# Attention heads on one core: PSUM banks dealt in the order of use, a multiplication and a split moved to other engines, two accumulators per block

## The reference, cut to what matters

```
q, k, v = the projections of the normalized input x     (scales folded into q and k)
s       = q @ k.T                      # 2048 x 2048 per head
m       = max over keys of s           # one per query, for a stable softmax
p       = exp(s - m)
o       = (p @ v) / sum over keys of p
x       = x + concat(o over heads) @ Wo + bo
```

## Time and profile before

| | before |
|---|---|
| median of 3 runs | 5179.72 us |
| the profiled execution's own time | 5180.22 us |
| its span, first to last instruction | 5178.5 us |
| PE busy | 4647.7 us (90%) |
| DVE busy | 2437.1 us (47%) |
| ACT busy | 1614.8 us (31%) |
| POOL busy | 1663.3 us (32%) |
| mean granted TensorE clock | 0.947 |
| the attention heads, first PE instruction to last DVE instruction | 1235.0 to 2225.7 us |

### The profile page before, as it was taken

How to read it: one execution, slowest core, us unless ns; L and a number is a source line. 1 busy time by engine, 2 the same in 40 slices (tenths; PEclk the granted TensorE clock), 3 DMA queues, 4 the chain that set the end, 5 groups by cost and what they waited for, 6 DMA issues and landing times. The chain is left out here.

```text
span 5178.5 us, 65784 instructions
## 1 busy us (share of the span) xinstructions
PE 4647.7 (90%) x26052; PEld 2578.8 (50%) x26052; DVE 2437.1 (47%) x3254; ACT 1614.8 (31%) x2764; POOL 1663.3 (32%) x1050
## 2 busy tenths in 40 slices
PE   6359997899999999977999869999999989789996
PEld 3124443333333333245666536666666658666663
DVE  7865888366666666852222223333333334512222
ACT  5414542212555555823111122222222220311110
POOL 2010001003888887023555401111111110145553
PEclk9679998999999999998999989999999999889998
DMA  2000000100000000026888720000000022468997
GB/s 73 0 15 7 6 0 35 35 1 1 1 1 1 1 1 1 1 96 191 259 251 260 176 99 23 31 31 31 23 31 29 23 82 84 160 190 259 259 258 196
DMA packets 237585, 417.69 MB, mean 81 GB/s; under 512 B 31472, under 2 KB 119536, under 8 KB 237296
## 3 DMA queue, kind: packets, MB, share of 16 engines
q1 hardware_dynamic: 179952, 270.89, 15.6%
q0 software_dynamic: 57344, 142.64, 11.3%
HBM read 297.53 MB, written 115.93 MB: 80 GB/s over the span
## 5 line engine op out<-in xcount | busy, mean ns | idle before, releaser
L2363 PE MATMUL linb_pr_ps<-lin_z,linb_wt 128*128 128x512 f32 x1536 | 677.7, 594 | 17.0 <-POOL linb_slope_own L2333 17.0
L1534 ACT ACTIVATE attc_prob<-attc_ps 128x512 f32<-128x512 f32 x1024 | 549.0, 596 | 425.7 <-PE attc_ps L1447 376.7
L1410 POOL TENSOR_TENSOR attc_acc<-attc_acc,attc_prob 128x2048 f32<-128x2048 f32 x144 | 651.5, 4524 | 68.7 <-ACT attc_prob L1534 51.2
L1558 DVE TENSOR_REDUCE attc_peak<-attc_ps 128x2 f32<-128x1024 f32 x384 | 469.7, 1226 | 256.6 <-PE attc_ps L1455 256.6
L1447 PE MATMUL attc_ps<-att_q,att_k 32*128 32x512 f32 x2048 | 528.6, 612 | 0.0
L2363 PEld LDWEIGHTS linb_pr_ps<-lin_z,linb_wt 128*128 128x128 f32 x1536 | 286.3, 191 | 342.5 <-issue 324.5
L1455 PE MATMUL attc_ps<-att_k,att_q 32*128 32x512 f32 x1536 | 443.6, 654 | 2.9 <-DVE attc_tot L1581 2.9
L2539 DVE SCALAR_TENSOR_TENSOR linb_gated<-linb_osb,linb_norm_w,linb_proj 128x512 f32<-128x512 f32 x64 | 94.4, 1474 | 668.1 <-ACT linb_osb L2466 668.1
L2340 POOL TENSOR_TENSOR linb_sq<-linb_osb 128x512 f32<-128x512 f32 x64 | 70.1, 1096 | 1039.6 <-ACT linb_osb L2466 1039.6
L1468 PE MATMUL attc_ps<-attc_prob,att_v 128*32 128x256 f32 (+1 forms) x3472 | 318.4, 439 | 0.3 <-ACT attc_prob L1534 0.3
L1074 DVE TENSOR_TENSOR_SCAN ssmb_state<-ssmb_decay,ssmb_bu 128x2048 f32<-128x2048 f32 x64 | 280.8, 4414 | 54.2 <-PE ssmb_y_ps L927 29.4
(11 more groups left out here) (462 smaller groups left out, 7591.0 us busy)
## 6 DMA issues: line engine op xcount, KB each, us to landing
moe1w_wgu<-in_L_ffn_gate_up_proj SPq DMA_DIRECT2D x32, 1536.0 KB
moe2w_wgu<-in_L_ffn_gate_up_proj SPq DMA_DIRECT2D x32, 1536.0 KB
moe1w_wd<-in_L_ffn_down_proj SPq DMA_DIRECT2D x32, 512.0 KB
gated_features<-linb_gated SPq DMA_DIRECT2D x64, 256.0 KB, 2.3
moe2w_wd<-in_L_ffn_down_proj SPq DMA_DIRECT2D x32, 512.0 KB
linc_gt<-gated_features SPq DMA_DIRECT2D x7, 2048.0 KB, 8.2
linb_wt<-in_L_attn_b_qkv_w SPq DMA_DIRECT2D x16, 768.0 KB, 4.6
residual_rows<-residual SPq DMA_DIRECT2D x8, 1024.0 KB, 4.3
```

The source lines that it names most:

```text
L1410: pool.tensor_tensor(acc[:, n % 2, :, :], before, prob[:, U % NP, :, :], ALU.add).then_inc(pool_done, 2 if at == 1 else 1)
L1534: nc.scalar.activation(prob[:, U % NP, h, :], ps[:, n % 3 if at < 0 else at % 6, :], ACT.Exp).then_inc(exp_done, 1)
L1558: V.tensor_reduce(peak[:, w // TT % 2, i % QH, 2 * hp:2 * hp + 2, b], ps[:, bank:bank + 2, :], axis=AX.X, op=ALU.max).then_inc(mx_used, 1)
L2363: last = nc.tensor.matmul(pr_ps[:, use % 2, :], wt[:, b, kind, k, :], z[:, k, t * NB:(t + 1) * NB], start=(k == 0), stop=(k == DT - 1))
```

## The change

All of it is in `attention_heads`:

- The banks 0 to 6 become one ring of seven. A planning loop numbers every use (a score, the maximum of one head, the sums, the rows) in the order in which PE comes to it, and records which semaphore count says that it is read. Use number x takes bank x mod 7 and waits for the release of use x - 7.
- Maxima are reduced head by head: four reductions of 128 x 512 a unit in place of two of 128 x 1024.
- The sums leave PSUM by an ACT copy into `tot` (two slots now); DVE takes the reciprocal in SBUF in four quarters of 128 columns, one in each of four successive units; the multiplication into `q` is done by POOL, after the addition of unit 6 of the next block.
- The split of the maxima: DVE only negates and reduces; ACT writes the high part, POOL subtracts for the low part.
- The accumulator of a block becomes two, for units 0 to 6 and units 7 to 13, in a ring of three. Units 0 and 1, and 7 and 8, are added together, so a block has 12 additions in place of 13, and `sums` has four sources in place of three.

The core of the diff:

```diff
...
+        HALF = 7
         SUMMED = (14, 15)
         POOLED = [i for i in range(TT) if i not in SUMMED]
-        acc = L.sb("acc", [P, 2, QH, NB])
-        tot = L.sb("tot", [P, NB])
+        acc = L.sb("acc", [P, 3, QH, NB])
+        tot = L.sb("tot", [P, 2, NB])
...
+        negs = neg[:, :].rearrange("p (i h) -> p i h", h=QH)
+        high, low = (negp[:, :, :].rearrange("p i (h r) -> p i h r", r=DH)[:, :, :, x] for x in range(2))
...
+            got = [("peak", h) for h in (2, 3, 0, 1)] if f < DT - 1 else []
+            if U >= LAG and (U - LAG) % TT == TT - 1:
+                got.append(("sums", 0))
+            if w % TT == 2 and ((f < DT - 1 and w > TT) or (0 < f < DT and w == 2)):
+                got.append(("rows", 0))
...
+        BANKS = 7
+        turn, released = {}, []
...
         for U in range(ALL + LAG):
+            pairs = [((0, 1), (2, 3)), ((2, 3), (0, 1))] if U < LAST_GROUP else [(range(QH), ())] if U < ALL else []
+            for scored, peaked in pairs:
+                for h in scored:
+                    turn["score", U, h] = len(released)
+                    released.append((exp_done, QH * U + h + 1))
+                for h in peaked:
+                    turn["peak", U, h] = len(released)
+                    peaks_and_rows += 1
+                    released.append((mx_used, peaks_and_rows))
+            for kind, _ in uses_of(U):
+                if kind == "sums":
+                    turn[kind, U] = len(released)
+                    row_sums += 1
+                    released.append((z_out, row_sums))
+                elif kind == "rows":
+                    turn[kind, U] = len(released)
+                    peaks_and_rows += 1
+                    released.append((mx_used, peaks_and_rows))
...
+        def accumulator(n, half):
+            return acc[:, (2 * n + half) % 3, :, :]
...
-            for n in range((DT - 1) * TC):
+
+            def split_low(n):
+                pool.wait_ge(high_done, n + 1)
+                pool.tensor_tensor(low, negs, high, ALU.subtract).then_inc(neg_done, 1)
+            def output(n):
+                f, t = n // TC, n % TC
+                pool.wait_ge(inverted, QH * (n + 1))
+                pool.wait_ge(o_out, n + 1)
+                pool.tensor_tensor(q[:, f, t * NB:(t + 1) * NB], o_raw[:, n % 2, :], tot[:, n % 2, :], ALU.mult).then_inc(o_used, 1)
+            def accumulate(n, at, i):
+                U = n * TT + i
+                pool.wait_ge(exp_done, (U + 1) * QH)
+                if at == 1 and n >= 2:
+                    pool.wait_ge(z_done, n - 1)
+                if at == HALF + 1 and n >= 1:
+                    pool.wait_ge(z_done, n)
+                if at % HALF >= 2:
+                    pool.wait_ge(pool_done, n * len(POOLED) + at)
+                to = accumulator(n, at // HALF)
+                before = prob[:, (U - 1) % NP, :, :] if at % HALF == 1 else to
+                pool.tensor_tensor(to, before, prob[:, U % NP, :, :], ALU.add).then_inc(pool_done, 2 if at % HALF == 1 else 1)
+
+            for n in range(DT * TC + 1):
+                if 1 <= n <= LAST_GROUP // TT:
+                    split_low(n - 1)
                 for at, i in enumerate(POOLED):
-                    if at == 0:
-                        continue
-                    U = n * TT + i
-                    pool.wait_ge(exp_done, (U + 1) * QH)
-                    if at == 1 and n >= 2:
-                        pool.wait_ge(z_done, n - 1)
-                    if at >= 2:
-                        pool.wait_ge(pool_done, n * len(POOLED) + at)
-                    before = prob[:, (U - 1) % NP, :, :] if at == 1 else acc[:, n % 2, :, :]
-                    pool.tensor_tensor(acc[:, n % 2, :, :], before, prob[:, U % NP, :, :], ALU.add).then_inc(pool_done, 2 if at == 1 else 1)
+                    if n < LAST_GROUP // TT and at % HALF:
+                        accumulate(n, at, i)
+                    if at == HALF - 1 and n >= 1:
+                        output(n - 1)
...
-            def take(U, kind):
-                n = use_at[U, kind]
-                if U >= LAST_GROUP:
-                    pe.wait_ge(mx_used, n)
-                elif n >= 2:
-                    pe.wait_ge(mx_used, n - 1)
...
+            def take(*what):
+                n = turn[what]
+                if n >= BANKS:
+                    sem, count = released[n - BANKS]
+                    pe.wait_ge(sem, count)
+                return n % BANKS
...
                 for h in heads:
-                    banks.append(score_bank(QH * U + h))
                     own = slice(h * DH, (h + 1) * DH)
-                    nc.tensor.matmul(ps[:, banks[-1], :], ones16[own, :], rows[own, cols], start=True, stop=False)
-                for h, bank in zip(heads, banks):
+                    nc.tensor.matmul(ps[:, take("score", U, h), :], ones16[own, :], rows[own, cols], start=True, stop=False)
...
-                bank = take(U, kind)
                 for h in heads:
                     own = slice(h * DH, (h + 1) * DH)
-                    last = nc.tensor.matmul(ps[:, bank + h % 2, :], q[own, f, i * P:(i + 1) * P], k[own, f, b * NB:(b + 1) * NB],
-                                            start=True, stop=True)
-                last.then_inc(mx_done, 1)
+                    nc.tensor.matmul(ps[:, take("peak", U, h), :], q[own, f, i * P:(i + 1) * P], k[own, f, b * NB:(b + 1) * NB],
+                                     start=True, stop=True).then_inc(mx_done, 1)
...
-                bank = take(U, kind)
+                bank = take("sums", U)
                 sem, count = summed_by(n - n % TT + POOLED[-1])
                 pe.wait_ge(sem, count)
-                sources = [prob[:, (n - 1) % NP, :, :], prob[:, n % NP, :, :], acc[:, n // TT % 2, :, :]]
+                sources = [prob[:, (n - 1) % NP, :, :], prob[:, n % NP, :, :], accumulator(n // TT, 0), accumulator(n // TT, 1)]
...
                 nc.scalar.copy(o_raw[:, n % 2, :], o_bank).then_inc(o_out, 1)
+                act.wait_ge(z_done, n + 1)
+                nc.scalar.copy(tot[:, n % 2, :], ps[:, bank_of(("sums", n * TT + TT - 1 + LAG)), :]).then_inc(z_out, 1)
+
+            def split_high(n):
+                act.wait_ge(negated, n + 1)
+                if n >= 1:
+                    act.wait_ge(mx_step, n)
+                nc.scalar.copy(high, negs).then_inc(high_done, 1)
...
+                if U % TT == 0 and 0 < U <= LAST_GROUP:
+                    split_high(U // TT - 1)
...
-                V.tensor_reduce(peak[:, w // TT % 2, i % QH, 2 * hp:2 * hp + 2, b], ps[:, bank:bank + 2, :],
+                dve.wait_ge(mx_done, use_count("peak", U, h))
+                V.tensor_reduce(peak[:, w // TT % 2, i % QH, h, b:b + 1], ps[:, bank_of(("peak", U, h)), :],
                                 axis=AX.X, op=ALU.max).then_inc(mx_used, 1)
...
+            def negate(U):
+                n = U // TT
+                dve.wait_ge(mx_used, use_count("peak", U, 1))
                 if n >= 1:
-                    dve.wait_ge(mx_step, n)
-                split_maxima(V, dve, neg, left_step, negp, peak[:, w // TT % 2], n, neg_done)
+                    dve.wait_ge(neg_done, n)
+                V.tensor_reduce(neg[:, :], peak[:, U % UNITS // TT % 2].rearrange("p i h b -> p (i h) b"),
+                                axis=AX.X, op=ALU.max, negate=True).then_inc(negated, 1)
...
-                V.reciprocal(tot[:, :], ps[:, bank, :]).then_inc(mx_used, 1)
-                dve.wait_ge(mx_used, use_at[U, "F"] + 1)
-                dve.wait_ge(o_out, n + 1)
-                f, t = n // TC, n % TC
-                V.tensor_tensor(q[:, f, t * NB:(t + 1) * NB], o_raw[:, n % 2, :], tot[:, :], ALU.mult).then_inc(o_used, 1)
+            def invert(n, step):
+                dve.wait_ge(z_out, n + 1)
+                part = tot[:, n % 2, step * P:(step + 1) * P]
+                V.reciprocal(part, part).then_inc(inverted, 1)
...
+                to = accumulator(n, at // HALF)
+                before = prob[:, (U - 1) % NP, :, :] if at % HALF == 1 else to
+                V.tensor_tensor(to, before, prob[:, U % NP, :, :], ALU.add).then_inc(vector_done, 2 if at % HALF == 1 else 1)
+
+            for U in range(ALL + LAG + QH):
+                if LAST_GROUP <= U < ALL and U % TT in POOLED and POOLED.index(U % TT) % HALF:
                     add(U)
...
+                if U < LAST_GROUP and U % TT == TT - 1:
+                    negate(U)
+                since = U - LAG - TT
+                if since >= 0 and since % TT < QH and since // TT < ALL // TT:
+                    invert(since // TT, since % TT)
...
```

More of the change, by code:

```diff
@@ L1382, in rows_block, with use_count @@
+        def use_count(*what):
+            return released[turn[what]][1]
         def rows_block(U):
@@ L1486, in turn_rows @@
                 pe.wait_ge(neg_done, rows_block(U) + 1)
-                bank = take(U, "R")
+                bank = take("rows", U)
```

(22 more changed lines are left out.)

91 lines of the change are left out of this document (19 added, 72 removed).

## The result

The changed kernel takes 5100.45 us (median of 4 runs, 5098.38 to 5103.71) against 5180.83 us before (4 runs, 5178.89 to 5184.23), a ratio of 0.9845 (95%: 0.9833 to 0.9856). Its profiled execution took 5098.89 us, span 5097.2. So the direction and the place were as forecast, and the gain was larger: 81.3 us between the two profiled executions, where the sum said 63.8.

The account below looks back on a forecast made before the run. POOL was taken to bound each block, its loop falling from 67.84 to 62.75 us. Eleven periods (-56.0), first block (-3.8), fourth group (-5.6) and tail (+1.6) gave -63.8 us, so 5116 us, range 5095 to 5150.

Parts of the forecast that it names:

- The rival in which the quarters are locked against GpSimd: Quarter reciprocals on DVE and POOL's additions hold each other up: period 71.8 us, 5225 us, chance 0.06.
- GpSimd's loop: POOL's additions, idle gaps and multiplication over one block, taken as the bound: 67.84 us before, 62.75 after.
- TensorE's line and the bound: PE's own work over one block, claimed 60.4 us, so POOL stays the bound with 2.3 us to spare on PE.
- signs of being wrong: Units of 3.76, a gap between additions of units 2 and 3, quarters or additions lengthening each other, or a PE-bound period.
- the ring: PE's wait for banks inside each unit disappears with seven banks: a unit goes from 3.76 to near 3.48 us.
- the ring still waits: Rival: the wait moves from rows to maxima, units stay at 3.76 us, +1.7 a block, 5137 us, chance 0.12.
- First block: No multiplication, one addition fewer and one more round of sums in the first block: -3.8 us.
- Fourth group: Units there fall from 2.38 to 2.18 us, partly lost to DVE's additions: gain 1.4 us a block, 5.6 in all.
- the tail: After the last sums, the copy, quarters, POOL's multiplication and signals replace DVE's reciprocal and multiplication: +1.6 us.
- The clock at the edges: Rival: PE's granted clock still falls to half after blocks' ends, 1.2 us back a block, 5130 us, chance 0.09.
- The gap before unit 3: POOL's wait for unit 3, caused by DVE's reciprocal holding the sums' bank, closes: 7.51 us become 4.65.
- The split: High and low parts of the negated maxima: cast (0.96 us) and subtraction leave DVE, POOL's low part costs nothing.

## Why the prediction was right, and where it was off

*The instructions' prices* came out as said. An addition takes 23.22 / 5 = 4.64 us (4.65 said), the multiplication 1.27 (1.26), the sums 3.55 (3.59), a reduction 0.681 (0.69) and a quarter 0.943 (0.84 to 0.96). The rival in which the quarters are locked against GpSimd falls: 895 to 954 ns in all 64, whatever GpSimd does.

*GpSimd's loop* was forecast at 62.75 us, and the block takes 62.33. From the additions of units 0 and 1 to that of unit 2 it stayed at 6.33 us (1432.32 - 1425.99), where the sum had 7.18 for the fourth round of sums. That round is there: with the old banks in the changed kernel the time is 7.14 us (1509.61 - 1502.47). The ring takes as much back, and the sum had left that out: the four exponentials of unit 2, which stood in two pairs with a wait between them, run as one. Before, then after:

```profile
1451.21 1.08 ACT L1534 ACTIVATE attc_prob<-attc_ps 128x512 f32<-128x512 f32 x2 [2.96 <-PE attc_ps L1447]
1453.03 1.08 ACT L1534 ACTIVATE attc_prob<-attc_ps 128x512 f32<-128x512 f32 x2 [0.73 <-PE attc_ps L1447]
```

```profile
1492.50 2.07 ACT L1557 ACTIVATE attc_prob<-attc_ps 128x512 f32<-128x512 f32 x4 [0.64 <-PE attc_ps L1473]
```

From unit 2 to unit 3 it closed to 5.07 us, not to 4.65.

*TensorE's line and the bound* are the step that failed, and two of the prediction's own signs of being wrong were seen: a period bound by TensorE, and idle time of GpSimd between units 2 and 3 (0.55 us). "PE's own line is ... 60.4 us, so POOL stays the bound, with 2.3 us to spare on PE": TensorE's line is 62.33 us, and GpSimd is the one with something to spare (0.4 us). The mis-sized term is the ring, "so the wait of today disappears and PE gets near 3.48 us a unit". It vanished in one half of two: 3.635 us a unit, so 14 x 0.155 = 2.2 us a block. The line's other terms, taken at the starts of ScalarE's exponentials, were 7.06 us for the unit with the sums (7.07 said) and 4.39 for the next (4.6). That the period came out right to 0.5 us is in part luck: the prices were right, but the line that was taken for the bound only happens to lie within 0.4 us of the one that is. The rival "the ring still waits" named the mechanism and priced it too high (3.76).

*First block*: -3.8 us forecast, -11.1 measured. What was missing is the clock. Before, TensorE paused in every unit and the granted clock stood at 0.50 until 1253; after, it does not pause, and the clock rises at about 1240 (windows of 3 us: width, busy time by engine, granted clock third from the end; after, then before).

```profile
1235.00:1238.00 3.00, 3.00 (x19) 2.01 (x18) 0.86 (x2) 1.62 (x3) 0.00 (x0) 0.50 0.00 0
1238.00:1241.00 3.00, 3.00 (x25) 2.34 (x21) 1.95 (x4) 2.04 (x5) 0.00 (x0) 0.78 0.00 0
1241.00:1244.00 3.00, 3.00 (x27) 1.75 (x22) 2.98 (x6) 2.49 (x5) 1.37 (x1) 1.00 0.00 0
```

```profile
1247.00:1250.00 3.00, 2.75 (x14) 0.90 (x11) 1.38 (x2) 1.08 (x2) 3.00 (x1) 0.50 0.00 0
```

With the old banks in the changed kernel that is lost again, and with the seven banks alone in the kernel before the clock is at 1.00 from 1241 on, so it belongs to the ring.

*Fourth group*: forecast -1.4 us a block, measured -2.7 (three periods between first additions, 38.7 against 41.4 us on average). From the twelfth block to the end of the stage it was -13.4 where the terms said about -9 (a period of -5.1, the fourth group's -5.6, the tail's +1.6). The unit fell from 2.38 to 2.18 us as said, but VectorE's additions hardly held it up. GpSimd's multiplication takes 3.19 us beside one of them and lengthens the next from 2.29 to 3.35 us, as the lock makes it, and ScalarE waits 0.24 us for it, not 0.5 to 1.1:

```profile
2043.34 2.22 DVE L1625 TENSOR_TENSOR attc_acc<-attc_acc,attc_prob 128x2048 f32<-128x2048 f32 x1
2043.50 3.19 POOL L1431 TENSOR_TENSOR att_q<-attc_o_raw,attc_tot 128x512 f32<-128x512 f32 x1 [36.33 <-DVE attc_tot L1612]
2045.48 3.35 DVE L1625 TENSOR_TENSOR attc_acc<-attc_prob 128x2048 f32<-128x2048 f32 x1
```

*The clock at the edges* did not fall; that rival is out. *The gap before unit 3* closed, and the whole reciprocal brings the stall back, so the cause that the prediction gave for it was right.

*The split* was counted as nothing ("the cast (0.96 us) and the subtraction leave DVE"). The sum took the cast off VectorE, so it was not hurt; but undoing the split costs 47 us, more than any other part. 0.96 us was the price of where the cast fell before, and the new order of work moves it. The split alone in the kernel before was not tried, so what it gives there is open.

## What to carry to other kernels

The five parts cost 166 us when undone one by one (3 + 33 + 40 + 43 + 47), and together they gave 80. Done alone, three of them changed the time by -13, -20 and +36 us. With several lines of work that lie within a microsecond or two of each other, the price of an edit depends on the others, and only the next bound says what it is worth. A short VectorE instruction that GpSimd's instructions can hold up, as the multiplication and the cast here, has no price of its own; what the trace shows (0.69 us, 0.96 us) is where it happened to fall, so add up to a whole GpSimd instruction to it whenever the change shifts it. And compute the second line to the hundredth: a term of 0.155 us, 14 times a block, decided which engine bound.

## What the runs showed of the hardware that was not expected

The same multiplication of 128 x 512 on VectorE took 0.69, 1.36, 4.09 and 5.03 us (medians) in four kernels that differ in what stands around it, and the cast 0.20 to 3.86 us. On GpSimd it took 1.27 us, but 3.19 beside an addition on VectorE. A reciprocal of 128 x 128 from SBUF to SBUF was never lengthened beside GpSimd's additions (895 to 954 ns). One pause of TensorE of 1.77 us was followed by about 6 us at half the clock, so such pauses cost 4.3 us a block (66.69 - 62.43) and not 1.77. Pauses of 1.17 and 1.46 us in the same kernel were not followed by a fall, and one of 1.33 us in another was.
